# Graph attention over 4096 nodes: the keys of all tiles first, then the values among the first head's score slots, with the normalised input read back

## The reference

```python
h = jnp.maximum(_layernorm(x, axis=-1), 0.0)
adj = jnp.maximum(adjacency_matrix, eye)
q = jnp.einsum('nd,hdk->hnk', h, Wqs)
k = jnp.einsum('nd,hdk->hnk', h, Wks)
v = jnp.einsum('nd,hdk->hnk', h, Wvs)
scores = jnp.einsum('hqk,hmk->hqm', q, k) * kd ** (-0.5)
scores = scores + 0.01 * eye - 1e16 * (1.0 - adj)
att = jax.nn.softmax(scores, axis=-1)
out = x + jnp.einsum('hqm,hmk,hko->qo', att, v, Wo)
```

## Time and profile before

| | |
|---|---|
| median of 3 executions | 2705.91 us (2703.6 to 2707.09) |
| profiled execution, its own time | 2709.6 us |
| its span | 2708.1 us |
| busy share of the span: PE, DVE, ACT, POOL | 97%, 83%, 68%, 47% |
| mean granted TensorE clock | 0.994 of full speed |
| group 0: first keys, first scores, first step | 12.95, 85.51, 101.10 us |
| group 1: first keys, first scores, first step | 1380.09, 1439.23, 1454.64 us |

### The profile page before, as it was taken

The page is one execution under the profiler, slowest core; times in us unless marked ns, Lnnn a source line. Parts: engine busy times, 40 slices in busy tenths (PEclk is TensorE's granted clock), DMA queues, the critical chain, the costliest instruction groups (busy, mean ns, idle before and its releaser), DMA issues. The chain is left out here.

```text
span 2708.1 us, 58752 instructions
## 1 busy us (share of the span) xinstructions
PE 2630.7 (97%) x17344; PEld 1901.9 (70%) x17344; DVE 2253.6 (83%) x3833; ACT 1850.8 (68%) x3041; POOL 1280.6 (47%) x2418
## 2 busy tenths in 40 slices
PE   7899999999999999999998999999999999999997
PEld 5666777767777776766766777777777777777775
DVE  6788888888888888888847888888888888888885
ACT  3576777767767676776745777777777777777774
POOL 2356655566565556655512444444444444343433
PEclk9999999999999999999999999999999999999999
DMA  6367766677776677776652566656565656555654
GB/s 163 111 143 177 184 163 175 165 168 167 173 190 170 164 177 166 171 171 169 167 142 76 146 158 151 158 142 145 138 151 145 164 146 162 133 146 138 157 144 106
DMA packets 263358, 418.51 MB, mean 155 GB/s; under 512 B 98944, under 2 KB 119936, under 8 KB 259200
## 3 DMA queue, kind: packets, MB, share of 16 engines
q1 hardware_dynamic: 172032, 228.88, 33.0%
q0 software_dynamic: 89088, 184.69, 29.7%
q10 hardware_dynamic: 2176, 4.19, 0.4%
HBM read 136.31 MB, written 46.27 MB: 67 GB/s over the span
## 5 line engine op out<-in xcount | busy, mean ns | idle before, releaser
L307 POOL DMA_DIRECT2D S<-S x2048 | 1007.8, 500 | 1137.1 <-DVE S L723 1089.6
L702 DVE CUSTOM_DVE_ANT_0 S<-psS,B 128x1024 f32<-128x1024 f32 x1024 | 1228.4, 1218 | 268.3 <-PE psS L449 155.1
L589 ACT ACTIVATE S<-S,negm 128x1024 f32<-128x1024 f32 (+1 forms) x768 | 1095.8, 1428 | 88.8 <-DVE negm L709 88.3
L596 ACT ACTIVATE PT<-psT 128x512 f32<-128x512 f32 x1024 | 595.0, 596 | 267.5 <-PE psT L462 248.5
L449 PE MATMUL psS<-K,QH 128*128 128x512 f32 x2048 | 729.2, 437 | 35.7 <-DVE mx L702 31.5
L449 PE MATMUL psS<-K,QL 128*128 128x512 f32 x2048 | 642.5, 395 | 0.0
L462 PEld LDWEIGHTS psT<-ident,S 128*128 128x128 f32 x4096 | 481.2, 140 | 192.0 <-issue 73.5
L462 PE MATMUL psT<-ident,S 128*128 128x128 f32 x4096 | 608.0, 276 | 7.8 <-ACT S L589 4.9
L723 DVE STREAM_TRANSPOSE S<-S 128x2048 f32<-128x2048 f32 x256 | 590.2, 2306 | 27.6 <-PE psO L486 23.7
L472 PE MATMUL psO<-PT,V 128*64 128x256 f32 x4096 | 492.1, 382 | 0.0
L486 PE MATMUL psO<-S,V 128*64 128x256 f32 x4096 | 470.3, 382 | 2.0 <-DMA S<-S 2.0
(11 more groups left out here) (51 smaller groups left out, 967.9 us busy)
## 6 DMA issues: line engine op xcount, KB each, us to landing
S<-S SPq DMA_DIRECT2D x2048, 64.0 KB, 3.1
S<-S POOLq DMA_DIRECT2D x2048, 64.0 KB, 2.9
B<-in_adj POOLq DMA_DIRECT2D x128, 256.0 KB, 7.2
bias_scratch<-B SPq DMA_DIRECT2D x32, 1024.0 KB, 5.8
B<-bias_scratch SPq DMA_DIRECT2D x128, 256.0 KB, 5.1
hq<-hT_scratch SPq DMA_DIRECT2D x32, 256.0 KB, 3.5
RB<-rden_scratch SPq DMA_DIRECT2D x128, 64.0 KB, 3.2
S<-in_x SPq DMA_DIRECT2D x8, 512.0 KB, 3.6
```

The lines of the kernel that those rows point to most:

```text
L307: pool.dma_start(dst, src).then_inc(late_sent[q][half], 16)
L589: nc.scalar.activation(part, part, ACT.Exp, bias=negm[:, h % 2, q:q + 1], accum_out=sums[:, h % 2, q, e:e + 1]).then_inc(probs_ready, 1)
L596: nc.scalar.activation(PT[:, s % RING, :], psT[s % 2][:, :], ACT.Copy).then_inc(pt_act, 1)
L702: nc.vector.tensor_tensor_reduce(out=part, in0=psS[j % 2][:, :], in1=B[:, q, k * SLOT:(k + 1) * SLOT], scale=SCALE, scalar=LOWEST, op0=ALU ...
```

## The change

- PE's loop over the tiles makes only the keys (and, in group 0, the transposes). The weights `Wk` alone are waited for; `Wv` is loaded behind the loop, into the buffer `res`, which the steps use later.
- The first query projection comes one tile earlier, into `psP` instead of `psT`.
- After the loop every tile of the normalised input is read again from `hT` by SP (`load_hv`, 512 KB each) into four buffers `hv`: two in a free part of `S`, two in `PT`. In group 1 each tile is thus loaded twice; in group 0 once, where it was never read back except for the queries.
- Values of tiles 0 to 3 come behind each pair of the first head's score slots, on PE, ACT and DVE alike; those of tiles 4 to 7 behind head 1's two slots.
- The two `transpose_late` of head 0 move: the first behind slot 5, the second behind head 1's slots.
- In group 1 the loads of the loop wait for the keys of the tile that had the buffer, not its values.

```diff
-        for w, dst in ((Wk, wk), (Wv, wv)):
...
+        def load_hv(n):
+
+            if norm:
+                sp.wait_ge(h_out[n % 2], 16 * (n // 2 + 1 + START))
+            sp.dma_start(hv[n % 4], hT[:, :, n * CH:(n + 1) * CH]).then_inc(hv_in[n % 4], 16)
+
+        load_weights(Wk, wk, w_in)
         load(0, 1)
...
                 if norm:
                     sp.wait_ge(x_transposed, i * 2 + b + 1)
                 else:
-                    sp.wait_ge(v_proj, i * 4 + (2 * b + 2 + START))
+                    sp.wait_ge(k_proj, i * GROUP + ((b + 1) * (GROUP // 2) + START))
                 load(i + 1, b)
...
+        load_weights(Wv, wv, wv_in)
+        for n in range(4):
+            load_hv(n)
+        for n in range(4, NC):
+            sp.wait_ge(v_proj, 2 * (n - 3) + START)
+            load_hv(n)
...
-            if not nxt:
+            if nxt and not nxt2:
                 pe.wait_ge(wqo_in, 16 * (DC + 2))
-                query(0, 0, True, True, first=True)
+                if not norm:
+                    pe.wait_ge(head_added_before, STEPS + START)
+                query(0, 0, True, True)
+
+        def value_rows(n):
+
+            pe.wait_ge(hv_in[n % 4], 16 * (n // 4 + 1))
             for u, read in ((0, v_act), (1, v_dve)):
...
-        pe.wait_ge(w_in, 16 * 2 * DC)
+        pe.wait_ge(w_in, 16 * DC)
...
         pe.wait_ge(k_lo, NC * GROUP + 2 * GROUP)
+        pe.wait_ge(wv_in, 16 * DC)
+        for n in range(SLOTS // 2):
+            scores(0, 0, 2 * n, True)
+            scores(0, 0, 2 * n + 1, True)
+            value_rows(n)
+        scores(0, 1, 0)
+        scores(0, 1, 1)
+        for n in range(SLOTS // 2, NC):
+            value_rows(n)
         pe.wait_ge(v_act, NC + START)
         pe.wait_ge(v_dve, NC + START)
-        for j in range(SLOTS):
-            scores(0, 0, j, True)
-        scores(0, 1, 0)
-        scores(0, 1, 1)
         steps(pe, step)
```

More of the change, by code:

```diff
@@ L103, in group_programs @@
          "k_proj", "v_proj", "k_hi", "k_lo", "v_act", "v_dve"))
+    wv_in = sem(f"wv_in{g}")
+    hv_in = [sem(f"hv_in{g}{b}") for b in range(4)]
     hq_in, base_in, stored = sem(f"hq_in{g}"), sem(f"base_in{g}"), sem(f"stored{g}")
@@ L212, in sync_program @@
             sp.wait_ge(projected_before, STEPS + START)
-        for c in range(DC):
-            sp.dma_start(wq[:, c, :].rearrange("p (h k) -> p h k", k=KD),
-                         Wq[heads, c * P:(c + 1) * P, :].rearrange("h p k -> p h k")).then_inc(wqo_in, 16)
+        load_weights(Wq, wq, wqo_in)
         Wo_v = Wo[heads, :, :].rearrange("(a e) k d -> e k a d", e=2)
@@ L236, in sync_program @@
         load_hq(0)
-        if norm:
-            for b in range(2):
-                sp.wait_ge(h_out[b], 16 * (NC // 2 + START))
+        if not norm:
+            sp.wait_ge(late_used_before, STEPS)
+            sp.wait_ge(pt_free_before, RING + STEPS * TS)
+            sp.wait_ge(stored_before, 16 * PAIRS)
+        load_weights(Wv, wv, wv_in)
[4 more added lines that the diff above has]
+            load_hv(n)
         sp.sem_inc(rden_stored, 16 * START)
@@ L421, in keys_values, with query @@
                     for c in range(DC):
-                        last = nc.tensor.matmul(psV[u][:, a * 256:(a + 1) * 256], hc[b][:, c, m * P:(m + 1) * P],
+                        last = nc.tensor.matmul(psV[u][:, a * 256:(a + 1) * 256], hv[n % 4][:, c, m * P:(m + 1) * P],
                                                 wv[:, c, :], start=(c == 0), stop=(c == DC - 1))
                 last.then_inc(v_proj, 1)
-        def query(i, h, wait_hq, free, first=False):
+        def query(i, h, wait_hq, free):
             if wait_hq:
@@ L433, in query @@
             for c in range(DC):
-                last = nc.tensor.matmul(query_psum(first)[:, 0:QW], wq[:, c, h * KD:(h + 2) * KD], hq[:, c, :],
+                last = nc.tensor.matmul(psP[:, 0:QW], wq[:, c, h * KD:(h + 2) * KD], hq[:, c, :],
                                         start=(c == 0), stop=(c == DC - 1))
@@ L529, in tensor_program @@
         pe.sem_inc(v_proj, START)
-        pe.wait_ge(w_in, 16 * 2 * DC)
+        pe.sem_inc(k_proj, START)
+        pe.wait_ge(w_in, 16 * DC)
         if norm:
@@ L568, in keys_values, with value_rows, query_hi @@
                 relu(*after(i, b))
[L569 to L572, removed]
+            if nxt and not nxt2:
+                query_hi(0, 0)
+        def value_rows(n):
+            act.wait_ge(v_proj, 2 * n + 1 + START)
+            nc.scalar.activation(V[:, n * CR:n * CR + 2, :], psV[0][:, :].rearrange("p (a n) -> p a n", a=2),
                                  ACT.Copy).then_inc(v_act, 1)
-        def query_hi(i, h, first=False):
+        def query_hi(i, h):
             act.wait_ge(q_proj, count(i, h, 1, 2))
@@ L579, in query_hi @@
                 for half_ in range(2):
-                    last = nc.scalar.activation(QH[half_ * KD:(half_ + 1) * KD, h + e, :], query_psum(first)[e * KD:(e + 1) * KD, 0:QW],
+                    last = nc.scalar.activation(QH[half_ * KD:(half_ + 1) * KD, h + e, :], psP[e * KD:(e + 1) * KD, 0:QW],
                                                 ACT.Copy)
@@ L635, in scalar_program @@
         act.sem_inc(pt_act, PT_START)
[L636 to L639, removed]
+        value_rows(0)
+        value_rows(1)
+        exps(0, 0, 0, 0)
+        exps(0, 0, 0, 1)
+        value_rows(2)
+        exps(0, 0, 0, 2)
+        value_rows(3)
+        exps(0, 0, 1, 0)
+        exps(0, 0, 1, 1)
+        for n in range(4, NC):
+            value_rows(n)
         steps(act, step)
@@ L672, in keys_values, with value_rows, query_lo @@
                                         ALU.subtract).then_inc(k_lo, 1)
-            if not nxt:
+            if nxt and not nxt2:
                 for e in range(2):
-                    query_lo(0, 0, e, True)
-            dve.wait_ge(v_proj, i * 4 + (2 * b + 2 + START))
-            nc.vector.tensor_copy(V[:, bass.ds((i * 2 + b) * CR + 2, 2), :],
+                    query_lo(0, 0, e)
+        def value_rows(n):
+            dve.wait_ge(v_proj, 2 * n + 2 + START)
+            nc.vector.tensor_copy(V[:, n * CR + 2:n * CR + 4, :],
                                   psV[1][:, :].rearrange("p (a n) -> p a n", a=2)).then_inc(v_dve, 1)
-        def query_lo(i, h, e, first=False):
+        def query_lo(i, h, e):
             dve.wait_ge(q_hi, count(i, h, 1, 2))
@@ L684, in query_lo @@
                 rows = slice(half_ * KD, (half_ + 1) * KD)
-                last = nc.vector.tensor_tensor(QL[rows, h + e, :], query_psum(first)[e * KD:(e + 1) * KD, 0:QW],
+                last = nc.vector.tensor_tensor(QL[rows, h + e, :], psP[e * KD:(e + 1) * KD, 0:QW],
                                                QH.bitcast(F32)[rows, h + e, :], ALU.subtract)
@@ L800, in vector_program @@
                 dve.wait_ge(h_out[b], 16 * (NC // 2 + START))
[L801 to L804, removed]
+        for n in range(SLOTS // 2):
+            mask(0, 0, 2 * n, first=True)
+            mask(0, 0, 2 * n + 1, first=True)
+            if n == 2:
+                transpose_late(0, 0, 0, False)
+            value_rows(n)
         mask(0, 1, 0)
         mask(0, 1, 1)
+        transpose_late(0, 0, 1, False)
+        for n in range(SLOTS // 2, NC):
+            value_rows(n)
         steps(dve, step)
```

28 lines of the change are left out of this document (16 added, 12 removed).

## The result

The changed kernel takes 2715.06 us in the median of 21 executions (2709.12 to 2721.95), beside 2706.37 us for the kernel before, timed with it. The ratio is 1.0039 (95% interval 1.0031 to 1.0048): slower by 10.5 us (8 to 13); the two medians lie 8.7 apart. One of the 21 executions of the kernel before took 7241.85 us and is left out of the ratio. Forecast were 2715.3 us and slower. Measured a second time the ratio was 1.005 (1.0033 to 1.0067).

What follows compares the result with a forecast made beforehand. PE was taken to bound the kernel, busy 97% of the span. Group 0 at 9.8 us longer and group 1 at 0.4 shorter gave 2705.9 + 9.4 = 2715.3 us for the median; range 2706 to 2728.

Steps and rivals of the forecast that it cites:

- The loop had to give back 19.3 us: Each group's loop must shorten by 19.3 us, as late values stand 52.6 behind first scores instead of 33.3.
- The next tiles at 49.55, 56.0 and 62.4: Group 0's loop: key starts of tiles 4 to 6, a tile costing 6.5 us instead of 7.76.
- Last tile's keys at 70.15: Group 0's loop: tile 7's keys start at 70.15 us after a stretched normalisation, before at 76.38.
- First scores at 76.0: Group 0: first scores start at 76.0 us against 85.51, giving back 9.5 of 19.3.
- The mixed stage 38.8: Behind the loop, both groups: scores with values take 38.8 us instead of 15.6 from first scores to first step.
- To the late values 13.8: First step, both groups: 13.8 us from its transposes to its late values instead of 17.7.
- half a megabyte more takes between 0 and its own 4.1; I take 1.4: Group 1's loop: tile 2's load lands 1.4 us after the last bias load (1390.6), so keys start at 1392.0.
- its term for group 1: Group 1: loop gives back 19.1 of 19.3 us, late values at 1472.7 instead of 1473.14; -0.4 in the total.
- Group 1's loads were not hidden: Rival in group 1's loop: tiles arrive within 3.45 us, scores 8.2 earlier, total +1.2, 2707 us; chance 0.18.
- PE did not stay at its low level: Rival in group 0's loop: low clock for three more tiles, +11, 2726 us; chance 0.17.
- The faster case: Rival in both groups: every input tile lands before it is wanted; total -6.4, 2699.5 us; chance 0.10.
- a change of pace in the steps: Sign of being wrong: the steps behind the prologues change pace; the forecast had them keep their length.

Runs made afterwards that it cites:

- The bias experiment: Changed kernel with group 1's eight bias loads issued behind the loop over the tiles; 1.0025 of the kernel before.
- the four buffers: Changed kernel with four input buffers in group 1, tiles 0 to 3 loaded ahead of the bias; 1.0017 of the kernel before, 1.0015 when repeated.
- the adjacency experiment: Changed kernel with group 0's eight adjacency loads issued behind tile 3's statistics instead of ahead of tile 2's; 1.0054 of the kernel before.
- the kernels with four tiles in the loop: Changed kernel with values of tiles 0 to 3 kept in group 0's loop: 1.0034 of the kernel before; with four input buffers in group 1 too: 0.9989.

## Why the prediction was right, and where it was not

**The mechanism in group 0 was right, step by step.** The loop had to give back 19.3 us and gave back 9.2 (76.29 against 85.51; 9.5 forecast). Normalising tile 3 at 36.0: 36.01. PE idle 5 us ahead of it: 6.23. Its keys at 40.8: 40.83. The next tiles at 49.55, 56.0 and 62.4: 48.85, 55.12 and 61.32; a tile cost 6.2 to 6.3, so the chain over the ReLU set the pace; DVE's normalisations came 6.5 apart (50.61, 57.12, 63.63) and fell behind, but did not hold PE within these three tiles. Last tile's keys at 70.15: 69.34, with the query's projection ahead of it and partly at the low level (1.60 and 4.82 us for 1.03 and 3.60). First scores at 76.0: 76.29. The last two agree in part by luck: the keys began 0.8 early, and the scores came 6.95 behind them, not 5.85, since PE fell to its low level at a place where the forecast had it at the full one. The mixed stage 38.8: 37.87 to the first transposes. To the late values 13.8: 13.94. Group 0 longer by 9.8: 9.3 in this pair, 9.8 in the mean of seven profiles against four (128.7 and 118.9).

**The stages behind the loop** did what the change means them to do. Late values stand 51.8 us behind the first scores, where they stood 33.3; 27.6 of values were put in for 18.5. The loads of the values cost nothing there: PE has under 0.8 us of idleness in the 37.80 us of the stage.

**Group 1 was mis-sized.** The step that failed is "half a megabyte more takes between 0 and its own 4.1; I take 1.4". From its issue to its use tile 2's transfer needed 8.6 us (1387.06 to 1395.68) where I had 6.6, and 7.2 to 7.7 in the four other profiles with this order. So 15.3 us lie between the first keys and tile 2's (14.2 to 14.3 in the others), where I had 13.0. The bias experiment shows the mechanism to be this queue. PE's wait was longer still, 8.12 us and not 4, because the first tile ran at the full level (7.13 us for two tiles) where I had it at the low one. After that PE waited 1.03 and 0.70 us for every second tile, about the 0.4 for each that I had. Later terms add: 4.7 from issue to landing instead of 4.1, a query input that held PE 1.36 us at 1418.60, and the query's low part ahead of the last rests on DVE. The first scores come 45.6 us after the first keys (44.0 to 44.7 in the others), instead of 41.1. Group 1 is 3.0 us longer in the mean (106.8 of five against 103.7 of three), not 0.4 shorter. The sum would then have been +12.8. Measured were 10.5 (8 to 13) and 13.5 (9 to 18). The forecast of 9.4 lies in both intervals although its term for group 1 had the wrong sign, because that term was off by only 3.4 us; that the forecast 2715.3 and the median 2715.06 agree to 0.3 us is luck.

**The rivals.** Group 1's loads were not hidden; the four buffers, with tiles 2 and 3 ahead of the bias, show what that is worth, 9 to 12 us of its stretch (95.15 to 98.19 in four profiles against 106.8). PE did not stay at its low level: 3.69 us for a tile's keys at 48.85 and after, with gaps of 1.7 us before each, and a granted clock of 1.00 from 48.8 to 67.0. It fell once, in 6.23 us of idleness, and again for a short time after 2.00 us at 67.02. The faster case had tile 3's load in time; in the adjacency experiment it was, and the wait went to another tile.

**What stays open.** The prediction named a change of pace in the steps as a sign of being wrong, and the profiles show one: the 63 steps of group 0 take 1239 to 1246 us behind the new prologue (seven profiles, mean 1242.8) and 1246 to 1252 behind the old or the half-changed one (six, mean 1249.5). About half of these 6.6 us is a matter of which execution was profiled. The six profiled executions with the long steps took 3.1 us more than the medians of their kernels in the mean, and the seven others 0.3 less; the kernel with four buffers shows both ends, with steps of 1239.4 us in an execution 10 us under its median and 1246.0 in one 10 us over it. What of the rest is real is open. Comparing times, the cost of the prologue is there in full, so it isn't that steps simply make up for a late start. DVE's waits for the moved blocks were 20 to 24 us in the first 24 steps in four profiles with the new prologue (27.2 in a fifth), and 22 to 34 in six with the old or mixed one, which goes the same way without telling a cause. Nor is it known why the kernels with four tiles in the loop are slower than their prologues. Both effects are nearly as large as what the change does to the time.

## What to carry to other kernels

Moving work out of a loop pays by the loop's shortening, and that is set by what bounds the loop once the work is gone: here a chain from PE over ACT and back in group 0 (7.76 to 6.3 us per tile for 3.45 of work taken out) and the transfers in group 1. Work that seems to be in the way may be what covers a latency; before taking it out, add up each chain without it. Where little but PE bounds the loop (group 1, with four buffers), the same move pays: 5 us faster than before when done there alone. The kernel before with four buffers and nothing else was not run, but in its group 1 PE has no idleness that more buffers could take away; its loop from tile 1 to the last values (length, then busy PE first; clock, DMA share and GB/s last):

```profile
1388.80:1438.00 49.20, 49.20 (x173) 32.47 (x171) 25.55 (x39) 22.29 (x39) 0.00 (x0) 1.00 0.26 83
```

When an order drops the work between two uses of a buffer, look at once at what stands ahead of that buffer's next load in its queue.

## What the runs showed of the hardware

The read of a 512 KB tile issued right behind eight loads of 256 KB on the same queue was in use 7.2 to 8.6 us later (five profiles; 1387.06 to 1395.68 in the changed kernel's first). With no such loads ahead of it, it was in use after 4.2 (1385.55 to 1389.78, one profile).

The other is the level of PE's clock. Windows of the changed kernel, each with the granted clock as the third number from the end:

```profile
37.40:39.40 2.00, 1.96 (x8) 1.57 (x8) 1.92 (x4) 0.00 (x0) 0.00 (x0) 0.50 0.00 0
48.80:67.00 18.20, 12.84 (x40) 6.15 (x40) 17.16 (x44) 9.27 (x16) 6.74 (x8) 1.00 0.84 282
76.30:86.80 10.50, 10.50 (x49) 9.03 (x49) 5.80 (x11) 1.96 (x3) 0.00 (x0) 1.00 0.16 51
1428.00:1430.00 2.00, 2.00 (x6) 1.53 (x6) 1.53 (x3) 0.00 (x0) 0.00 (x0) 0.50 0.00 0
```

Repeated gaps of 1.7 us in each 6.2 us left it at the full level (second row); gaps of 6.23 us (first row) and, in the adjacency kernel, of 7.12 us did not. In between the length of a gap doesn't tell. Behind 2.00 us (at 67.02), 2.87 (at 1426.00; fourth row) and 3.13 and 3.23 us (in front of the first scores of the kernels with four tiles in the loop and with four buffers), the first 0.5 to 1.3 us of work were at the full level, and then the clock fell to the low one. Behind 2.13 us (at 76.29; third row) and 3.16 us in front of the adjacency kernel's first scores they were not.
